# Moving the small jobs within a batch, two engines and two DMA queues for the first batch's operands, and paired maxima pieces in step 0

## What is computed

```python
xn = layernorm(x)
q, k, v = split(xn @ w_in.T + b_in)              # 16 heads of width 8
scores = q @ k.T / sqrt(8); only |i - j| <= 128 allowed
attn = softmax(scores)                           # float32 reference
attn_out = xn + (attn @ v) @ w_out.T + b_out
x_q = clip(round(xn / xscale), -128, 127)        # int8 product
ffn = (x_q @ wq.T) * xscale * wscale + fbias
x1 = x + attn_out + ffn
```

## Time and profile before

| what | value |
|---|---|
| median of three runs | 728.19 us |
| profiled execution: time, span | 732.44 us, 730.4 us |
| PE busy | 575.6 us (79% of the span) |
| DVE, ACT, POOL busy | 465.4, 341.5, 316.1 us |
| mean granted PE clock | 0.942 of full speed |
| first scores of layer 0 | 63.6 us |
| last x1 of layer 0 | 431.6 us |

### The profile page before, as it was taken

One profiled execution on the slowest core, in us unless ns is written; L12 is line 12 of the kernel. 1 busy time (PEld: TensorE's weight loads), 2 busy tenths in 40 slices (PEclk: granted clock), 3 DMA queues, 4 the chain that ended last, 5 costly groups with the idle time before them and its releaser, 6 DMA issues. The chain is left out here.

```text
span 730.4 us, 18096 instructions
## 1 busy us (share of the span) xinstructions
PE 575.6 (79%) x5741; PEld 360.6 (49%) x5742; DVE 465.4 (64%) x1896; ACT 341.5 (47%) x1037; POOL 316.1 (43%) x361
## 2 busy tenths in 40 slices
PE   2378887888888978889799849988972699999930
PEld 0135554555554545555465426666542366666620
DVE  3688767686777776766777037888875254445425
ACT  2202563654645646447466635655641244444410
POOL 6950533443332435423100014788874155555530
PEclk9999999999999999999999989999987699999975
DMA  2845036171381542702600223111211122222209
GB/s 58 176 99 103 31 81 125 31 162 46 74 160 32 119 87 59 169 25 69 136 18 18 75 77 149 57 58 45 71 54 49 34 74 76 73 76 73 76 15 345
DMA packets 51140, 61.18 MB, mean 84 GB/s; under 512 B 9841, under 2 KB 41973, under 8 KB 49280
## 3 DMA queue, kind: packets, MB, share of 16 engines
q1 hardware_dynamic: 45568, 49.73, 29.2%
q0 software_dynamic: 4352, 8.47, 3.5%
q10 hardware_dynamic: 1152, 2.10, 0.7%
HBM read 32.08 MB, written 28.45 MB: 83 GB/s over the span
## 5 line engine op out<-in xcount | busy, mean ns | idle before, releaser
L571 DVE CUSTOM_DVE_ANT_0 A<-A,band 128x320 f32<-128x320 f32 (+2 forms) x512 | 213.7, 467 | 92.6 <-PE A L729 91.7
L464 ACT ACTIVATE Pb<-SB 128x320 f32<-128x320 f32 (+2 forms) x512 | 176.2, 403 | 162.2 <-PE SB L759 159.0
L729 PE MATMUL A<-Ks,Qs 48*64 48x320 bf16 (+2 forms) x1024 | 151.3, 303 | 10.9 <-DVE mneg L571 9.7
L750 PE MATMUL SB<-Qs,Ks 50*64 50x320 bf16 (+2 forms) x1024 | 145.9, 290 | 3.6 <-ACT Pb L464 2.9
L759 PE MATMUL SB<-ends,ident 64*64 64x64 bf16 (+1 forms) x1024 | 106.7, 206 | 0.0
L1518 POOL DMA_INDIRECT results<-y,xt x72 | 70.7, 982 | 71.5 <-issue 37.6
L750 PEld LDWEIGHTS SB<-Qs,Ks 50*64 50x64 bf16 x1024 | 57.0, 107 | 58.5 <-issue 29.5
L729 PEld LDWEIGHTS A<-Ks,Qs 48*64 48x64 bf16 x1024 | 57.6, 110 | 48.5 <-DVE mneg L571 36.1
L1622 PE MATMUL UP<-w_up,xT 128*128 x144 | 80.1, 639 | 1.7 <-ACT xT L1531 1.2
L770 PE MATMUL PV<-Pb,Va 128*32 128x320 f32 (+2 forms) x1024 | 77.2, 422 | 0.0
L1080 POOL DMA_INDIRECT expert_rows<-pay,pos x64 | 62.9, 983 | 24.0 <-issue 17.8
(11 more groups left out here) (194 smaller groups left out, 973.4 us busy)
## 6 DMA issues: line engine op xcount, KB each, us to landing
Qs<-parts_dram SPq DMA_DIRECT2D x16, 384.0 KB, 6.1
Ks<-parts_dram SPq DMA_DIRECT2D x16, 384.0 KB, 8.9
xt<-expert_rows SPq DMA_DIRECT2D x72, 65.0 KB, 1.8
yb<-results SPq DMA_DIRECT2D x8, 512.0 KB, 6.8
parts_dram<-qp SPq DMA_DIRECT2D x16, 192.0 KB, 2.8
parts_dram<-kp SPq DMA_DIRECT2D x16, 192.0 KB, 2.8
l_xb<-x_dram SPq DMA_DIRECT2D x9, 256.0 KB, 3.0
xb<-in_x SPq DMA_DIRECT2D x8, 256.0 KB, 3.0
```

Source lines behind the costliest of these rows:

```text
L464: act.activation(Pb[:, group % 4, c, 0:w], SB[k % NB_BANKS][:, 0:w], ACT.Exp).then_inc(act_exp, 1)
L571: nc.vector.tensor_tensor_reduce(scores_of, scores_of, band[:, skip:skip + w], -1.0, 3e38, ALU.add, ALU.min, mneg[:, step % 2, col:col + 1 ...
L729: mm = nc.tensor.matmul(A[k % NA_BANKS][r0:r0 + HP, 0:w], Qs[b % RING][rows, a, HP * sub:HP * sub + HP], Ks[b % RING][rows, a, lo:lo + w], ...
L750: nc.tensor.matmul(out[r0:r0 + HP, 0:w], Ks[b % RING][rows, a, HP * sub:HP * sub + HP], Qs[b % RING][rows, a, lo:lo + w], start=True, stop ...
```

## The change

The numbers `u` of the small jobs change on all engines at once; their order on `misc` changes with them. `LEAD` = 16 becomes `LATE` = 12: before the first slot no piece of step 1 is made; in step 0 of batch 0 slots 0 to 15 carry two pieces each (all of step 1), slots 16 to 31 carry 20 pieces of step 2, and from then on pieces run 20 ahead of a step. For batch 0 the normalization goes from POOL to DVE, the split of k to DVE and its store to ACT's queue, as do four row loads; q and k get PSUM banks of their own. Batch g+1's statistics, normalization and load of x move ahead of batch g's last jobs.

```diff
-LEAD = UNITS // 2
+LATE = 12
-    def ahead(step, v):
-        return (step + 1, LEAD + v) if v < LEAD else (step + 2, v - LEAD)
+    def ahead(b, u):
+        step, v = STEPS * b + u // UNITS, u % UNITS
+        if step == 0:
+            pieces = [(1, 2 * v), (1, 2 * v + 1)] if v < HG * 4 else [(2, n) for n in range(
+                (v - HG * 4) * (UNITS - LATE) // (HG * 4), (v - HG * 4 + 1) * (UNITS - LATE) // (HG * 4))]
+        else:
+            pieces = [(step + 1, UNITS - LATE + v) if v < LATE else (step + 2, v - LATE)]
+        return [piece for piece in pieces if piece[0] < NSTEP]
...
             place_max(STEPS * b + 1)
+            if g < NB:
+                store_parts(g, 0)
+                store_parts(g, 1)
+                load(g)
+            if g + 1 < NB:
+                load_x(g + 1)
             if b > 0:
                 sp.wait_ge(dve_x1, b)
                 sp.dma_start(x1v[b - 1], x1s[:]).then_inc(dma_x1, 16)
-            if g + 1 < NB:
-                load_x(g + 1)
-            if g < NB:
-                store_parts(g, 0)
             if b + 1 < NB:
                 place_max(STEPS * b + 2)
             if g < NB:
-                store_parts(g, 1)
-                load(g)
                 sp.wait_ge(pool_b2, g + 1)
...
         for g in range(2, NB):
-            rstd_of(g)
-            norm(g)
-            base_x(g)
-            quant_scale(g)
-            quant_clip(g)
-            quant_int(g)
             for which in range(2):
                 rest(g, which)
                 second(g, which)
                 third(g, which)
+            quant_scale(g)
+            quant_clip(g)
+            quant_int(g)
             base_bias(g)
+            if g + 1 < NB:
+                rstd_of(g + 1)
+                norm(g + 1)
+                base_x(g + 1)
             base_ffn(g)
...
+        def norm_0():
+            dve.wait_ge(pool_rs, 1)
+            for i in range(NT):
+                nc.vector.tensor_scalar(xn[:, i, :], xb[:, i, :], mv[:, i, 0:1], rstd[:, i:i + 1],
+                                        ALU.subtract, ALU.mult).then_inc(dve_xn, 1)
+        def k_parts_0():
+            dve.wait_ge(act_kf, 1)
+            dve.wait_ge(act_k1, 1)
+            nc.vector.tensor_tensor(rk[:], kf[:], kp[:, 0, :], ALU.subtract).then_inc(dve_rk, 1)
+            dve.wait_ge(dve_rk, 1)
+            nc.vector.tensor_copy(kp[:, 1, :], rk[:]).then_inc(dve_k2, 1)
+            dve.wait_ge(dve_k2, 1)
+            nc.vector.tensor_tensor(kp[:, 2, :], rk[:], kp[:, 1, :], ALU.subtract).then_inc(dve_k3, 1)
...
-                if u == 8 and b + 1 < NB:
+                if u == 4 and b + 1 < NB:
                     evac_v(b + 1)
                 if b > 0:
-                    if u == 12:
+                    if u == 28:
                         context(b - 1, 0, misc)
-                    if u == 17:
+                    if u == 34:
                         context(b - 1, 1, misc)
-                    if u == 29:
+                    if u == 44:
                         out_x1(b - 1)
                 if g < NB:
-                    if u < NT:
-                        bn(g, u)
-                    if u == NT:
-                        ag(g)
...
+                if g + 1 < NB:
+                    if 50 <= u < 50 + NT:
+                        bn(g + 1, u - 50)
+                    if u == 50 + NT:
+                        ag(g + 1)
```

More of the change, by code:

```diff
@@ L612, in _ @@
         ag(0)
+        norm_0()
         absmax(0)
         scales(0)
+        fill(0)
+        for i in range(NT):
+            bn(1, i)
+        ag(1)
+        k_parts_0()
         dve.wait_ge(dma_rows, 16 * 6)
@@ L681, in _, with turn_xn, project @@
     def _(pe):
-        def turn_xn(g, before):
-            pe.wait_ge(pool_xn, NT * (g + 1))
-            pe.wait_ge(*before)
+        def turn_xn(g, before, bank=misc):
+            if g == 0:
+                pe.wait_ge(dve_xn, NT)
+            else:
+                pe.wait_ge(pool_xn, NT * g)
+            if before:
+                pe.wait_ge(*before)
             for i in range(NT):
-                mm = nc.tensor.transpose(misc[:, i * P:(i + 1) * P], xn[:, i, :], ident[:])
+                mm = nc.tensor.transpose(bank[:, i * P:(i + 1) * P], xn[:, i, :], ident[:])
             mm.then_inc(pe_xnT, 1)
-        def project(g, which, done, before):
+        def project(g, which, done, before, bank=misc):
             pe.wait_ge(act_xnT, g + 1)
-            pe.wait_ge(*before)
-            nc.tensor.matmul(misc[:], w_in[:, which * P:(which + 1) * P], xnT[g % 2][:], start=True, stop=True)\
+            if before:
+                pe.wait_ge(*before)
+            nc.tensor.matmul(bank[:], w_in[:, which * P:(which + 1) * P], xnT[g % 2][:], start=True, stop=True)\
                 .then_inc(done, 1)
@@ L823, in _ @@
                 scores(b, u)
[L824 to L825 removed]
+                for step, n in ahead(b, u):
                     piece(step, n)
[L827 to L852 removed]
                 if u % 8 == 2:
@@ L857, in _ @@
                             attend(group // NS, group % NS)
+                if u == 3 and b + 1 < NB:
+                    values(b + 1, (dve_ffn, NT * (b + 2)))
+                if u == (17 if b > 0 else 21):
+                    turn_max(STEPS * b + 1, (act_q1, g + 1) if g < NB else
+                             (dve_v, 4 * (b + 2)) if b + 1 < NB else (act_mT, STEPS * b + 1))
+                if b > 0:
+                    if u == 27:
+                        turn_ctx(b - 1, 0, misc, (act_k1, g + 1) if g < NB else (act_mT, STEPS * b + 2))
+                    if u == 33:
+                        turn_ctx(b - 1, 1, misc, (dve_ctx, 2 * b - 1))
+                    if u == 39:
+                        turn_ctxn(b - 1, (dve_ctx, 2 * b))
+                    if u == 43:
+                        out_mm(b - 1)
+                if u == 48 and b + 1 < NB:
+                    turn_max(STEPS * b + 2, (dve_x1, b) if b > 0 else (act_k1, g + 1))
+                if g < NB:
+                    if u == 9:
+                        turn_xn(g, (dve_v, 4 * (b + 2)))
+                    if u == 13:
+                        project(g, 0, pe_q, (act_xnT, g + 1))
+                    if u == (21 if b > 0 else 25):
+                        project(g, 1, pe_k, (act_mT, STEPS * b + 2))
+                    if u == 53:
+                        turn_xq(g, (act_mT, STEPS * b + 3))
+                    if u == 58:
+                        ffn_mm(g, (act_xqT, g + 1))
         for sub in (NS - 2, NS - 1):
```

231 lines of the change are left out of this document (112 added, 119 removed).

## The result

The changed kernel takes **754.9 us** (median of 4 runs, 752.5 to 759.8) against 728.6 (727.3 to 732.0): ratio **1.035**, 95% interval 1.031 to 1.040. It is 26 us slower where I forecast 7 us faster. The profiled execution of the changed kernel has a span of 751.1 us at a mean granted clock of 0.887, that of before 730.4 at 0.942. All that follows is layer 0.

The account below looks back on a forecast made before the run. PE was taken to set the 47.8 us steady batch, losing 6.2 us to waits. Terms: +3.3 (batch 1 later), -4 x 0.5, -3.0, -2.7, -2.2 = -6.6 us, giving 721.6 us against a 728.2 median; range 706 to 734.

Parts of the forecast that it names:

- start: Before first scores: DVE normalization and earlier stores bring scores at 58.4 instead of 63.6, 5.2 us won.
- batch 0: 84 pieces instead of 64 cost 0.8 us, late x at slot 50 costs PE 7.7; batch 1 begins 3.3 us later.
- batches 1 to 4: Steady batches: 3.0 us won from waits, 2.5 lost to late x, so 0.5 us won in each.
- batches 5, 6, 7: Batches that load no x: 3.0, 2.7 and 2.2 us won from removed waits.
- PE loses 2.5 us. Of 3.0 us won, 0.5 remain: Slot 50, batches 1 to 4: DVE waits 3.3 us for x, three full banks and a product cover part.
- the slower rival: Slots 50 to 58, batches 0 to 4: x at upper bound, stop takes the clock; 740 us, chance 0.14.
- The 3.0 us won: Steady batch: of 6.2 us of PE waits only 3.2 stay after the jobs move to new slots.
- The three that I had named: PE waits left in a steady batch: values' copy 1.6 us, q's evacuation 0.93, first context 0.65.
- my 44.8: Period in us of a steady batch after 3.0 us won, before the cost of late x.
- The load chain: From `project` of k to x landing: split 5.5, stores 4.0, loads 11.5, sum 21.0 us; DVE reaches slot 50 in 17.7.
- The moved waits: Steady batch: PE's waits for context (1.46), maxima (0.49) and x1 (0.76) go; q's stays; copy's becomes a bank wait.
- half of 0.16 and nearly all of 0.14: Chances of two rivals: x in time, 706 us (0.16), and slower, 740 us (0.14).

Follow-up runs that it names:

- the version with x early: Changed kernel with x of batch g+1 loaded ahead of the odd step's maxima rows and all parts, not behind the stacked loads: 728.9 us, ratio 0.999.
- The version with PE kept busy: Changed kernel, x still late, with dummy matmuls on PE at slots 54 to 57 while DVE waits for x: 752.1 us median (743.6 to 755.8).
- the single execution above: Changed kernel with x early, no pairs, and SyncE instead of ACT loading the four rows: run once, stacked loads landed at 36.5 us instead of 38.4.
- Taking the pairs away: Changed kernel with 20 pieces of step 1 made before the first slot, one per slot after: 751.6 us, ratio 1.029; with x early too, 0.996.
- spreading the copy alone: Changed kernel with x early and no pairs, values' copy split one instruction each behind the maxima of slots 4 to 7: ratio 0.992.

## Why the prediction was wrong

Its own steps, against the two traces:

| | predicted | measured | |
|---|---|---|---|
| start | -5.2 | -1.9 | scores at 61.9, not 58.4 |
| batch 0 | +8.5 | +15.9 | |
| batches 1 to 4 | -2.0 | +10.4 | 4 x 3.1 apart |
| batches 5, 6, 7 | -7.9 | -4.5 | |
| sum | -6.6 | +19.9 | |

**The failed step is "PE loses 2.5 us. Of 3.0 us won, 0.5 remain".** It prices a stop at its length and puts the clock behind it at nothing. The standing itself was even shorter than forecast: PE stood 7.5, 1.8, 1.6, 1.8 and 2.7 us at the five stops, 15.4 in all, where 7.7 and 4 x 2.5 make 17.7. What lacks is the clock. From the first product with the values of batch 0 to that of batch 7, in the change and in the version with x early (length, PE busy):

```profile
76.15:414.56 338.41, 289.31 (x3815) 0.92 0.37 77
77.09:387.65 310.56, 276.67 (x3814) 0.97 0.39 84
```

They are 27.9 us apart. 15.2 us of it PE stood, and 12.6 us it was busy longer with the same work (x is the number of its instructions in the trace) at a lower clock. So a late x costs nearly as much again in clock as in standing. In batch 2 it is 0.75 us between slots 50 and 58, 1.55 between 58 and 2, and 1.55 more between 2 and 10, where the clock had come back and fell again. I knew the mechanism and had put it into the slower rival alone, at 1.1 us a batch, with a stop of 5 us as its condition. PE's stop of 1.6 us at 214 was enough. The version with PE kept busy shows that the low clock up to slot 2 comes of PE standing in that stop: with matmuls in it the clock stays up. That the falls at slot 2 come of the stop is not shown. They stand at the start of three of batches 1 to 5 in the change, with PE kept busy too, and of one of five with x early.

**The 3.0 us won were too many as well, and the match of 45.05 with my 44.8 is luck.** My count let the clock fall once in a batch as before, and the batch of 45.05 us has no such fall. In it PE's waits sum to 5.2 us, against 7.3 before: 2.0 us won. The three that I had named came as counted (1.25, 1.04 and 0.69 us; I had 1.6, 0.93 and 0.65). But five short waits at the banks and at SB add 2.3 us, where before has 1.2 of them, and I had counted none. The rest of the 2.75 us is the clock. Per batch, 1 to 4, the change takes 50.4 us where I had 47.3: 2.6 of these 3.1 us is PE busy longer (42.9 us against 40.35), 0.5 is PE standing longer than I said.

**Batches 5 and 6** took 1.5 and 2.9 us more than with x early (42.3 us for batch 6, against 39.4). In both the clock falls, at slot 2 in batch 6, and no x is waited for in either. Batch 6 takes 42.3 us in all five traces of the changed kernel with a late x, and 39.4 or less in six of the seven with x early. That is hardly chance, but the waits of PE ahead of it are the same in both, and no run shows the link.

**The rival that came closest** is the slower one, 740. Its place, slots 50 to 58, was right. Its condition, x landing about 13 us behind the first load, was nearly met (12.3 to 13.1), but a PE stop of 5 us was not needed for the clock to fall; its price for the clock, 1.1 us a batch, was less than half of the 2.6.

**The load chain was right to about 1 us, and two errors cancel in it.** In batch 2 it took 21.8 us from the end of `project` of k to x's use where I had 21.0, and DVE reached slot 50 after 18.8 us where I had 17.7. So its wait came out at 3.0 for 3.3; in batch 0 it was 8.9 for 8.6.

**The moved waits** went where I put them. Context, maxima and x1 are gone, q's stayed, the copy's became one for a maximum.

**The start** was 3.3 us too good. The stacked loads land at 37.2, not 34.5. Of these 2.7 us ACT's row loads make 1.5 to 1.9 (the single execution above). My 3.1 MB at the 185 GB/s of the earlier trace rows are 17 us, not the 15 to 16 that I wrote; how much of the rest that is no run shows (the same code landed between 37.2 and 38.7). PE then waits for GpSimd's quantization (2.8 us), which the forecast had.

**Batch 0** is 7.4 us longer than I said. From the first scores to batch 1 the change takes 9.7 us more than the version with x early, 7.7 by my count of the stop; PE stood 7.5 us, and the 2 us are the clock behind the long stop (0.50 from 114 to 120). The other 5 are in that version too: it takes 52.8 us to slot 2, where my count comes to 47.4 (the 46.55 of before, 63.82 to 110.37, and 0.8). Taking the pairs away gives 2.4 to 3.4 of them back. That my count let too much of the twenty extra maxima pass in PE's shadow fits this, but is not shown.

**The range.** It leaves out half of 0.16 and nearly all of 0.14, which is 0.22 and not under 2 in 10.

What stays open: why the same stop of 1.2 us takes the clock in one batch and not in the next, and why it falls at slot 2 more often with a late x. The Trainium skill ("TensorE: Matmul & The Clock Gate", Part 1) calls the window in which the chip watches PE free-running, and explains by it that the moment of warming up varies. That the place of a gap in that window decides about a fall in the same way is my guess; none of the runs tests it, and batch 6 speaks for something less random.

## What to carry to other kernels

- Before moving a load behind others in a queue, add up the chain to its reader; here that sum was right to about 1 us in a steady batch. A small transfer that DVE waits for goes ahead of the bulk, not behind.
- Price a stop of the tensor engine at its length and then the stretch behind it at the lower clock. Here 15 us of standing came with 12.6 us of low clock.
- Compare two periods only when both have the same low stretches of the clock in them; a period of 45.05 us looked like 2.75 us won, and the average of four batches showed 0.85.
- When a copy blocks a bank, look for its next reader: here spreading the copy alone moved the stop, and most of the gain came when the reader of the bank moved too.

## What the runs showed of the hardware

- Behind a stop of 1.6 us the granted clock stays at 0.50 for almost 7 us though PE is busy 2.00 of 2.00 us. It was down behind waits of 0.57, 0.68 and 0.23 us within 2 us, and once stayed up behind 1.25 us.
- A 256 KB read that is issued behind two pairs of stacked loads is in use 9.0 to 10.7 us later (five batches of the change, and five of the kernel before with x late).
- Matmuls whose result nobody reads, issued through the stop, kept the granted clock at 1.00 behind it in five of five batches.
- The part of the program behind layer 0, untouched, took 300 us in the first runs and 330 to 337 in the later ones, with the same kernel text.
